# Two layer biases and the mask's alpha, added by accumulating DMAs instead of by VectorE

## The chip, the cores and the metric

The kernel runs on one core of one Trainium2 chip. The metric is the device time of one execution in microseconds (us); smaller is better. Time before: 1246.89 us, the median of 3 runs (1245.54 to 1247.73).

## What is computed

The input is x, 8 batches of 1024 nodes with 128 features in fp32, and one adjacency matrix adj, 1024 x 1024, mostly zero. Four graph layers follow one another, each with a residual and a layer norm:

```python
x = layernorm(x + (adj @ (x @ W0) + b0))                    # layer 0
x = layernorm(x + L1(x, adj))                               # layer 1: adj @ x and a rank-two term, @ W1, + b1
x = layernorm(x + L2(x, adj))                               # layer 2: attention
x = layernorm(x + L3(x, adj, 5 steps))                      # layer 3: gated recurrence
# layer 2
x_h = elu(x @ Wi + bi)
e = sigmoid(a_tgt[:, :, None] + a_src[:, None, :] + be)     # 1024 x 1024 for each batch
mask = adj + ALPHA * (1 - (adj != 0))                       # ALPHA = 0.005
e = e * mask
recv = elu(concat([e @ x_h, x_h * e.sum(-1)]) @ Wn + bn)
out = concat([recv, x_h]) @ Wm + bm
# layer 3, five times
m = adj @ h;  z = sigmoid(...m, h...);  r = sigmoid(...);  hv = tanh(...m, r*h...);  h = (1 - z)*h + z*hv
```

## The kernel before, in words

Products with adj are exact to about fp32: adj and x are split into a high and a low part (`adj_hi`, `adj_lo`, `xh`, `xl`), and each product is three passes of TensorE (`adj_product`, L700). One 128 x 1024 row tile of adj^T is loaded into each of eight buffers, `stage[0..7]` (fh, fr, fk, fz, hT0, hT1, r, v), which later hold the attention's and the recurrence's data. ScalarE makes `adj_hi` from a stage, VectorE `adj_lo`.

The **mask** of layer 2 is made from the same stages. VectorE computes `noedge = (stage == 0) * ALPHA` (L1237) into two slots of the ring, then `stage = stage + noedge` in place (L1239), and SyncE (the queue SP) stores the stage to a scratch in DRAM, `mask_scratch` (L621). SP loads no piece of the mask before all eight stores are in (`s_mstore`), and ScalarE waits for the same before its first attention copy, `t2a:0`, since that overwrites fh.

The four recurrences' pairs of batches (0 and 1, 2 and 3, 4 and 5, 6 and 7) run one after another. A pair has 5 steps of 2 batches, so there are 40 **units**, 0 to 39. A unit's TensorE work is two state products of 24 matmuls (128x512) and its gates. Layers 0 to 2 of each batch are cut into **pieces**, and `TABLES` at the head of the file lists for each engine in which order it runs them: lines `first` run ahead of unit 0, a line `unit5 @7 y0a:4` puts piece y0a of batch 4 into slot 7 of unit 5. Every engine runs its own list strictly in order and waits on semaphores for what it needs. The pieces that matter here (b is the batch):

- `x0` splits x (ScalarE, VectorE L1177). `m0a, m0b` are layer 0's adj products (half a and half b of the nodes, 24 matmuls each), `m1a, m1b` layer 1's. ScalarE copies each out of PSUM.
- `c0` (VectorE, L1258): x += b0 over 128 x 1024, after `xl0`. `c2`: x += bm, likewise, after ScalarE has copied the turned x (`tca`, `tcb`). `y0, y1, y2`: TensorE's small products (L718), and VectorE adds them to x (L1265); y0 waits for c0's, y2 for c2's signal.
- `v0, v1, v2` are norm statistics on VectorE (L1185 to L1203), `n0, n1, n2` the power -1/2 and a product on GpSimd (L659, L661) and eight applications on ScalarE (L979). n0 is followed by a new split: `xh1` on ScalarE, `l1` on VectorE.
- `d1` is two sets of row dots on VectorE (L1207), `sums` and `rows` the rank-two term of layer 1 (TensorE L759, L766, VectorE L1280 to L1298).
- Attention: `t2` turns x (L711), `pj` is x @ Wi with its elu (L778; VectorE L1305, L1308), `th` and `tg` (L711, L789), `as` (row dots). `s00..s17` are the 16 tiles of e: a sigmoid on ScalarE (L1029), on VectorE a product with a mask piece (L1326) and a running sum (L1333); `e00..e17` is the product on TensorE (L797). A mask piece (`k00..k17`) is loaded by SP into one of RING = 3 slots. `rs`, `rv`, `y2` end the attention.

The first list holds all of layers 0 and 1 of batches 0 to 2 and most of the attention of batches 0 and 1. GpSimd (POOL) has three loads of small vectors, the constants, and then only the n pieces and the output norms.

Of the kernel before, what the change touches and what calls it, by code (L numbers as in the profile page):

```python
# [81 lines left out]
unit0 @2 e10:1 e11:1 e12:1 @5 e13:1 @6 e14:1 e15:1 @7 e16:1 @8 pja:2 pjb:2 m1a:3 e17:1 m1b:3 rsa:1 sums:3 rsb:1 tha:2 rows:3 y1a:3 rva:1 y1b:3 @10 thb:2 tga:2 rvb:1 tgb:2 @13 y2a:1 @15 y2b:1 @20 e00:2 e01:2 e02:2 @25 e03:2 e04:2 e05:2 e06:2
unit1 @10 e07:2 @22 rsa:2 e10:2 e11:2 rva:2
unit2 @8 y2a:2 @15 e12:2 @22 e13:2 e14:2 e15:2
unit3 @22 e16:2 e17:2 rsb:2
unit4 @12 rvb:2 @21 y2b:2 @25 t2a:3
unit5 @13 t2b:3 pja:3 pjb:3 @18 tha:3 @19 thb:3 tga:3 @25 tgb:3
unit6 @11 e00:3 e01:3 @17 e02:3 @21 e03:3 @22 e04:3 e05:3
unit7 @11 e06:3 e07:3 @13 rsa:3 @22 e10:3
unit8 @6 e11:3 @9 e12:3 e13:3 e14:3 rva:3 @21 y2a:3 @22 e15:3 e16:3 e17:3  # L90
unit9 @27 rsb:3
unit10 @2 rvb:3 @10 y2b:3 @18 m0a:4 @20 m0b:4
unit11 @1 y0a:4 @3 y0b:4 @22 m1a:4 @24 m1b:4
unit12 @9 sums:4 @13 rows:4 @18 y1a:4 @21 y1b:4
unit13 @10 t2a:4 t2b:4 @12 pja:4 pjb:4 @17 tha:4 @18 thb:4 tga:4 m0a:5 tgb:4 m0b:5 e00:4 e01:4 @22 e02:4 e03:4 e04:4 y0a:5 e05:4
unit14 @2 e06:4 @6 y0b:5 e07:4 @8 rsa:4 @10 rva:4 e10:4 @15 e11:4 @16 e12:4 @19 y2a:4 e13:4 m1a:5 e14:4 @21 e15:4
unit15 @11 m1b:5 @12 e16:4 e17:4 sums:5 rsb:4 @13 rows:5 @14 rvb:4 @15 y1a:5 @19 y1b:5 y2b:4
unit16 @10 t2a:5 t2b:5 @16 pja:5 pjb:5 @21 tha:5 @22 thb:5 tga:5 @26 tgb:5
unit17 @10 e00:5 @11 e01:5 @17 e02:5 @18 e03:5 @19 e04:5 e05:5 @23 e06:5 @24 e07:5 @26 rsa:5 e10:5 e11:5
unit18 @1 rva:5 e12:5 e13:5 @8 y2a:5 e14:5 e15:5 e16:5 @9 e17:5 @11 rsb:5 @15 rvb:5 @22 y2b:5  # L100
# [4 lines left out]
unit23 @10 t2a:6 t2b:6 @13 pja:6 pjb:6 @17 m0a:7 tha:6 thb:6 m0b:7 tga:6 tgb:6 y0a:7 @19 y0b:7 @21 e00:6 @22 e01:6
unit24 @8 e02:6 e03:6 e04:6 @11 e05:6 @14 m1a:7 e06:6 @16 e07:6 @18 rsa:6 @22 m1b:7 rva:6 @26 sums:7
unit25 @12 rows:7 e10:6 e11:6 e12:6 y2a:6 @22 y1a:7 e13:6 e14:6
unit26 @1 e15:6 @3 y1b:7 e16:6 e17:6 @5 rsb:6 @10 rvb:6 @19 y2b:6 @23 t2a:7 t2b:7
unit27 @13 pja:7 pjb:7 @18 tha:7 @19 thb:7 tga:7 @22 tgb:7
unit28 @1 e00:7 @9 e01:7 @11 e02:7 @17 e03:7 @18 e04:7 @19 e05:7 e06:7 @23 e07:7 @25 rsa:7 e10:7 e11:7 @26 e12:7 @27 rva:7 e13:7 e14:7  # L110
# [19 lines left out]
unit1 @0 s07:2 @6 e07:2 s10:2 s11:2 s12:2 @8 s13:2 s14:2 @11 rva:2  # L130
unit2 @6 s15:2 @8 s16:2 s17:2
unit3 @8 e17:2
unit4 @6 rvb:2 @16 n2:2
unit5 @6 t2a:3 t2b:3 pja:3 pjb:3 tha:3 @8 thb:3 tga:3 @11 tgb:3 s00:3 @16 s01:3 s02:3
unit6 @6 s03:3 s04:3 s05:3 @8 s06:3 @10 s07:3
unit7 @6 e07:3 s10:3 s11:3 s12:3 @10 s13:3 @16 s14:3
unit8 @5 s15:3 s16:3 s17:3 rva:3 @11 e17:3
unit9
unit10 @1 rvb:3 @6 x0:4 m0a:4 n2:3 @11 m0b:4
unit11 @6 n0:4 @10 m1a:4 @11 m1b:4  # L140
unit12 @16 n1:4
unit13 @6 t2a:4 t2b:4 x0:5 pja:4 pjb:4 tha:4 @7 thb:4 tga:4 m0a:5 tgb:4 s00:4 s01:4 s02:4 m0b:5 s03:4 s04:4 @10 s05:4 s06:4 s07:4 @16 e07:4 s10:4 s11:4
unit14 @3 s12:4 @6 n0:5 rva:4 s13:4 @7 s14:4 @9 s15:4 s16:4 s17:4 m1a:5
unit15 @6 m1b:5 @7 e17:4 rvb:4 @16 n1:5
unit16 @6 n2:4 t2a:5 t2b:5 pja:5 pjb:5 @8 tha:5 @11 thb:5 tga:5 @12 tgb:5 @16 s00:5 s01:5 s02:5
unit17 @6 s03:5 s04:5 s05:5 s06:5 @8 s07:5 @11 e07:5 s10:5 s11:5 @12 s12:5 s13:5 s14:5 @16 rva:5 s15:5 s16:5
unit18 @3 s17:5 @5 e17:5 @6 rvb:5 @16 n2:5
unit19
unit20 @6 x0:6 @11 m0a:6 @12 m0b:6
# [2 lines left out]
unit23 @6 x0:7 t2a:6 t2b:6 pja:6 pjb:6 @7 m0a:7 tha:6 thb:6 m0b:7 tga:6 tgb:6 s00:6 @9 s01:6 s02:6 @10 s03:6 s04:6
unit24 @3 s05:6 n0:7 @6 s06:6 s07:6 @7 e07:6 s10:6 s11:6 s12:6 m1a:7 @10 m1b:7 rva:6
unit25 @6 s13:6 s14:6 s15:6 @10 s16:6 s17:6 @16 e17:6
unit26 @6 n1:7 rvb:6 @16 n2:6
unit27 @6 t2a:7 t2b:7 pja:7 pjb:7 tha:7 @8 thb:7 tga:7 @11 tgb:7 s00:7 @16 s01:7 s02:7
unit28 @5 s03:7 s04:7 @6 s05:7 s06:7 s07:7 @11 e07:7 s10:7 s11:7 s12:7 s13:7 s14:7 @12 s15:7 @16 rva:7 s16:7 s17:7
# [18 lines left out]
first s06:1 s07:1
unit0 @0 y0a:3 y0b:3 s10:1 s11:1 s12:1 v0:3 s13:1 s14:1 s15:1 s16:1 c2:2 l1:3 @2 s17:1 d1:3 pja:2 pjb:2 rsa:1 sums:3 rsb:1 rows:3 rva:1 y1a:3 y1b:3 as:2 rvb:1 v1:3 y2a:1 s00:2 s01:2 s02:2 y2b:1 v2:1 @4 s03:2 s04:2 s05:2 @9 s06:2
unit1 @0 s07:2 @4 s10:2 s11:2 s12:2 rsa:2 @6 s13:2 @7 s14:2 rva:2
unit2 @1 y2a:2 @4 s15:2 @6 s16:2 @7 s17:2
unit3 @7 rsb:2  # L180
unit4 @4 rvb:2 @6 y2b:2 @7 v2:2
unit5 @4 c2:3 pja:3 pjb:3 @6 as:3 @7 s00:3 @15 s01:3
unit6 @4 s02:3 s03:3 s04:3 s05:3 @6 s06:3 @7 s07:3
# [1345 lines left out]
```

## Time and profile before

| | |
|---|---|
| median of 3 runs | 1246.89 us (1245.54 to 1247.73) |
| the profiled execution | 1247.9 us, its span 1246.1 us |
| TensorE busy | 1200.8 us, 96% of the span |
| VectorE busy | 902.5 us, 72% |
| ScalarE busy | 678.7 us, 54% |
| GpSimd busy | 74.8 us, 6% |
| mean granted TensorE clock | 0.989 |

The span is the time from the first to the last instruction; 1.8 us of the profiled execution lie around it. Busy times of engines overlap, so what matters is where TensorE stands idle, and which engine's late result ends that idle time. A granted clock of 1.00 is TensorE at 2.4 GHz, and 0.5 would be 1.2 GHz; a stretch between the two spent part of its time at each.

### The profile page before, as it was taken

The numbers are of one execution on the slowest core, as the hardware profiler recorded it, in microseconds if no ns is written. First come the engines' busy times: TensorE is split into PE (matmuls) and PEld (weight loads), VectorE is DVE, ScalarE is ACT, GpSimd is POOL, SyncE is SP. The second block draws the span as 40 slices with busy tenths as digits, with TensorE's granted clock in tenths as the row PEclk, the third lists the DMA queues.
The fourth block names the chain that finished last, engine by engine and source line by source line (L and its number), as shares of the span: only waits on it lengthen the run. The fifth ranks groups of instructions, "written<-read, shape, count | busy, mean of one in ns | idle before, by whom it ended". The sixth has DMA issues, their size and how long they took to land.

```text
span 1246.1 us, 15438 instructions
## 1 busy us (share of the span) xinstructions
PE 1200.8 (96%) x5296; PEld 917.8 (74%) x5296; DVE 902.5 (72%) x2085; ACT 678.7 (54%) x1107; POOL 74.8 (6%) x79
## 2 busy tenths in 40 slices
...
GB/s 247 161 1 61 101 102 32 53 110 51 66 103 77 60 34 68 35 60 100 79 30 99 109 3 40 60 58 53 85 77 36 105 72 18 17 1 1 1 1 34
DMA packets 73038, 77.90 MB, mean 63 GB/s; under 512 B 6592, under 2 KB 48064, under 8 KB 72960
## 3 DMA queue, kind: packets, MB, share of 16 engines
...
## 4 chain that ended last, share of the span: by engine, by line
PE 77%; DVE 10%; ACT 4%; issue 3%; SPq 2%; DMA 2%; POOL 1%; DVEq 0%; POOLq 0%; ACTq 0%
PE ps L700 43%; PE ps L705 6%; PE ps L707 6%; PE ps L706 6%; PE ps L797 4%; PE ps L718 4%; PE ps L711 2%; DVE ring L1326 2%; DMA tl<-state_scratch 2%; ACT x L979 1%; SPq L588 1%; PE ps L810 1%; PE ps L778 1%; PE ps L803 1%; PE ps L789 1%
## 5 line engine op out<-in xcount | busy, mean ns | idle before, releaser
L700 PE MATMUL ps<-adj_hi,xh 128*128 128x512 f32 x672 | 288.5, 429 | 8.5 <-DVE xl L1177 6.2
L700 PE MATMUL ps<-adj_hi,xl 128*128 128x512 f32 x672 | 264.5, 394 | 0.0
L700 PE MATMUL ps<-adj_lo,xh 128*128 128x512 f32 x672 | 264.0, 393 | 0.0
L700 PEld LDWEIGHTS ps<-adj_hi,xh 128*128 128x128 f32 x672 | 127.6, 190 | 46.4 <-issue 16.0
L700 PEld LDWEIGHTS ps<-adj_lo,xh 128*128 128x128 f32 x672 | 127.7, 190 | 34.8 <-issue 11.3
L700 PEld LDWEIGHTS ps<-adj_hi,xl 128*128 128x128 f32 x672 | 127.3, 189 | 27.9
L797 PE MATMUL ps<-ring,fz 128*128 128x512 f32 x224 | 110.9, 603 | 3.5 <-DVE ring L1326 3.5
L1351 DVE TENSOR_TENSOR r<-r,hT 128x512 f32<-128x512 f32 x80 | 54.1, 690 | 78.7 <-ACT r L1089 78.5
L705 PE MATMUL ps<-mh,wh 128*128 128x512 f32 x240 | 104.2, 434 | 2.0 <-DVE ml L1177 1.5
L1177 DVE TENSOR_TENSOR ml<-ps,mh 128x512 fp32r<-128x512 f32 x80 | 55.0, 688 | 69.4 <-ACT mh L974 69.4
L974 ACT ACTIVATE mh<-ps 128x512 fp32r<-128x512 f32 x80 | 47.2, 591 | 104.2 <-PE ps L700 103.9
L1326 DVE TENSOR_TENSOR ring<-ring,mk 128x512 f32<-128x512 f32 x128 | 86.8, 682 | 21.6 <-ACT ring L1029 21.4
L1029 ACT ACTIVATE ring<-fh,asrcm 128x512 f32<-128x512 f32 x112 | 76.9, 718 | 39.0 <-PE ps L797 33.7
L707 PE MATMUL ps<-ml,wh 128*128 128x512 f32 x240 | 93.9, 391 | 0.0
L706 PE MATMUL ps<-mh,wl 128*128 128x512 f32 x240 | 93.6, 390 | 0.0
L974 ACT ACTIVATE xh<-tl 128x512 fp32r<-128x512 f32 x48 | 30.2, 630 | 99.7 <-DMA tl<-state_scratch 99.7
L1089 ACT ACTIVATE r<-ps,cols 128x512 f32<-128x512 f32 x80 | 54.5, 688 | 40.8 <-PE ps L707 40.5
L705 PE MATMUL ps<-th,wh 128*128 128x512 f32 x160 | 70.9, 443 | 2.7 <-DVE tl L1177 2.7
L1081 ACT ACTIVATE z<-ps,cols 128x512 f32<-128x512 f32 x80 | 53.6, 685 | 28.1 <-PE ps L707 27.8
L797 PEld LDWEIGHTS ps<-ring,fz 128*128 128x128 f32 x224 | 40.3, 190 | 38.7 <-issue 16.8
L1333 DVE TENSOR_TENSOR fr<-fr,ring 128x512 f32<-128x512 f32 x84 | 58.2, 692 | 8.8
L707 PE MATMUL ps<-tl,wh 128*128 128x512 f32 x160 | 62.6, 391 | 0.0
...
## 6 DMA issues: line engine op xcount, KB each, us to landing
mk<-mask_scratch SPq DMA_DIRECT2D x128, 256.0 KB, 2.8
...
x<-in_x SPq DMA_DIRECT2D x8, 512.0 KB, 4.1
out<-x SPq DMA_DIRECT2D x7, 512.0 KB, 3.2
hT<-in_adjT SPq DMA_DIRECT2D x2, 512.0 KB, 10.4
mask_scratch<-hT SPq DMA_DIRECT2D x2, 512.0 KB, 2.6
fh<-in_adjT SPq DMA_DIRECT2D x1, 512.0 KB, 5.0
```

The lines of the kernel that those rows point to most:

```text
L700: mm = pe.matmul(dst, a[:, t, :], b[:, t, cut(h)], start=(t == 0 and i == 0), stop=(t == T - 1 and i == 2))
L705: pe.matmul(dst, wh[:, k, :], hi, start=first, stop=False, skip_group_check=True)
L706: pe.matmul(dst, wl[:, k, :], hi, start=False, stop=False, skip_group_check=True)
L707: return pe.matmul(dst, wh[:, k, :], lo, start=False, stop=last, skip_group_check=True)
L797: tell(pe.matmul(ps[:, BANKS_B[b][h], :], f["z"][:, tile(t)], ring[:, place[b, h, t] % RING, :], start=(t == 0), stop=(t == T - 1)), "ag" ...
L974: return act.activation(dst, src, ACT.Copy)
L1029: tell(act.activation(ring[:, k % RING, :], f["h"][:, cut(h)], ACT.Sigmoid, bias=f["asrc"][:, t:t + 1]), "sg" + name[1:], b)
L1089: act.activation(r[:, cut(h)], ps[:, GB + h, :], ACT.Sigmoid, bias=rb).then_inc(r_done, 1)
L1177: return dve.tensor_tensor(dst, src, hi.bitcast(F32), ALU.subtract)
L1326: tell(dve.tensor_tensor(ring[:, k % RING, :], ring[:, k % RING, :], mk[:, k % RING, :], ALU.mult), "ma" + name[1:], b)
L1333: tell(dve.tensor_tensor(f["r"][:, cut(h)], first_sum, ring[:, k % RING, :], ALU.add), "rs_" + name[1:], b)
L1351: dve.tensor_tensor(r[:, cut(h)], r[:, cut(h)], hT[s][:, cut(h)], ALU.mult).then_inc(rh_done, 1)
```

## The change

- The VectorE pieces c0 and c2 are gone. GpSimd's queue issues for each of them a DMA that adds to x in SBUF (`accum_op=ALU.add`) from a scratch in DRAM, `bias_dram`, in which two small DMAs at the start repeat b0 and bm eight times to a row of 1024. y0 and y2 wait for the DMA's semaphore (`biased`).
- The mask: SP stores each raw stage to `mask_scratch` right after the weights' loads. VectorE waits for that store and then turns the stage in place into `(stage == 0) * ALPHA` (one instruction for two). GpSimd's queue issues a DMA that adds the stage to `mask_scratch`; its landing counts in `s_mstore`.
- GpSimd no longer waits for the last `adj_lo` before its list.
- All five lists are written anew: the order of pieces in `first` and their unit and slot.

```diff
     "PE": """
-first m0a:0 m0b:0 y0a:0 y0b:0 m0a:1 m0b:1 y0a:1 m0a:2 m1a:0 m1b:0 sums:0 y0b:1 m0b:2 rows:0 y1a:0 y0a:2
-first y0b:2 y1b:0 m1a:1 m1b:1 sums:1 t2a:0 t2b:0 rows:1 y1a:1 y1b:1 pja:0 pjb:0 m1a:2 tha:0 thb:0 m1b:2
-first tga:0 tgb:0 t2a:1 sums:2 t2b:1 rows:2 pja:1 e00:0 y1a:2 e01:0 e02:0 pjb:1 y1b:2 e03:0 e04:0 e05:0
...
+first m0a:0 m0b:0 m0a:1 y0a:0 y0b:0 m0b:1 y0a:1 y0b:1 m0a:2 m0b:2 m1a:0 m1b:0 sums:0 m1a:1 rows:0 y1a:0
+first m1b:1 y1b:0 sums:1 y0a:2 y0b:2 rows:1 y1a:1 y1b:1 t2a:0 t2b:0 pja:0 pjb:0 tha:0 thb:0 tga:0 tgb:0
+first m1a:2 t2a:1 m1b:2 e00:0 e01:0 e02:0 e03:0 t2b:1 e04:0 sums:2 pja:1 e05:0 e06:0 e07:0 rows:2 y1a:2
...
     "ACT": """
-unit0 @0 e07:1 s10:1 s11:1 s12:1 t2a:2 t2b:2 @1 s13:1 s14:1 s15:1 @2 s16:1 n0:3 @4 s17:1 pja:2 pjb:2 e17:1 m1a:3 m1b:3 tha:2 rva:1 thb:2 tga:2 rvb:1 tgb:2 s00:2 s01:2 s02:2 n1:3 @8 s03:2 s04:2 s05:2 @9 n2:1 @11 s06:2
+unit0 @0 s16:1 s17:1 t2a:2 e17:1 t2b:2 pja:2 pjb:2 @1 n0:3 rva:1 tha:2 @2 thb:2 m1a:3 rvb:1 m1b:3 @4 tga:2 tgb:2 s00:2 s01:2 s02:2 n2:1 @8 s03:2 s04:2 n1:3 @9 s05:2 @10 s06:2 @11 s07:2
...
     "DVE": """
-first x0:0 c0:0 x0:1 x0:2 y0a:0 c0:1 y0b:0 weights:0 v0:0 mask:0 c0:2 mask:1 y0a:1 mask:2 l1:0 d1:0 mask:3
-first mask:4 mask:5 mask:6 mask:7 y0b:1 sums:0 v0:1 rows:0 y0a:2 y1a:0 y1b:0 l1:1 v1:0 d1:1 y0b:2 v0:2
...
+first x0:0 x0:1 x0:2 weights:0 mask:0 mask:1 mask:2 mask:3 mask:4 mask:5 y0a:0 y0b:0 mask:6 v0:0 y0a:1 y0b:1
+first mask:7 v0:1 l1:0 d1:0 l1:1 d1:1 sums:0 rows:0 y1a:0 y1b:0 v1:0 sums:1 y0a:2 y0b:2 rows:1 v0:2 y1a:1
+first y1b:1 v1:1 pja:0 pjb:0 l1:2 as:0 d1:2 s00:0 s01:0 s02:0 s03:0 s04:0 s05:0 s06:0 s07:0 sums:2 pja:1
...
-unit18 @1 s16:5 s17:5 y2a:5 @4 rsb:5 rvb:5 @7 y2b:5 v2:5
-unit19
-unit20 @5 x0:6 @9 c0:6 @13 y0a:6 @15 y0b:6 v0:6
+unit18 @4 pja:5 pjb:5 @7 as:5 @15 s00:5
+unit19 @4 s01:5 s02:5 s03:5 s04:5 @5 s05:5 s06:5 s07:5 @9 s10:5 s11:5 @10 s12:5 s13:5 @13 s14:5 @15 rsa:5 s15:5 s16:5 s17:5 rva:5
+unit20 @2 y2a:5 rsb:5 x0:6 @4 rvb:5 y2b:5 v2:5 @11 y0a:6 @15 y0b:6 v0:6
...
     "POOL": """
-first n0:0 n0:1 n1:0 n0:2 n1:1 n1:2 n2:0 n0:3 n1:3 n2:1 n2:2
+first c0:0 c0:1 c0:2 mask:0 mask:1 mask:2 mask:3 mask:4 mask:5 mask:6 n0:0 mask:7 n0:1 n1:0 c2:0 n0:2 n1:1
+first c2:1 n1:2 c0:3 n2:0 c2:2 n0:3 n2:1 n1:3 n2:2 c2:3 n2:3
...
+        def biased(b, n):
+
+            return s_xb[b // 2 % 2][b % 2], 32 * (b // 4) + (16 if n == "0" else 32)
...
-            for n, t in enumerate(t for piece, t in order["DVE"] if piece == "mask"):
-                sp.wait_ge(s_mask, n + 1)
-                sp.dma_start(mask_dram[tile(t), :], stage[t]).then_inc(s_mstore, 16)
+            for t in range(T):
+                sp.wait_ge(s_adj[t], 16)
+                sp.dma_start(mask_dram[tile(t), :], stage[t]).then_inc(s_adj[t], 16)
...
+            for n, c in enumerate((0, 2)):
+                pool.dma_start(bias_dram[n:n + 1, :].rearrange("o (t d) -> o t d", d=D),
+                               w["rows"][:, c * D:(c + 1) * D].unsqueeze(1).to_broadcast([1, T, D])
+                               ).then_inc(s_rep, 16)
...
+                if name == "mask":
+                    pool.wait_ge(s_mask, 1 + [t for piece, t in order["DVE"] if piece == "mask"].index(b))
+                    pool.dma_start(mask_dram[tile(b), :], stage[b], accum_op=ALU.add).then_inc(s_mstore, 16)
                     return
                 f = set_of(name, b)
-                if name in ("n0", "n1", "n2"):
+                if name in ("c0", "c2"):
+                    pool.wait_ge(s_rep, 32)
+                    for e in ("xl0",) if name == "c0" else ("tca", "tcb"):
+                        seen(pool, e, b)
+                    n = int(name == "c2")
+                    pool.dma_start(x_of(b)[:, :, :].rearrange("p t d -> p (t d)"),
+                                   bias_dram[n:n + 1, :].to_broadcast([P, N]), accum_op=ALU.add
+                                   ).then_inc(biased(b, name[1])[0], 16)
+                elif name in ("n0", "n1", "n2"):
...
-            pool.wait_ge(s_al, T)
...
             def mask(t):
...
                 dve.wait_ge(s_al, t + 1)
-                dve.tensor_scalar(noedge, stage[t], 0.0, ALPHA, ALU.is_equal, ALU.mult).then_inc(s_noedge, 1)
-                dve.wait_ge(s_noedge, n + 1)
-                dve.tensor_tensor(stage[t], stage[t], noedge, ALU.add).then_inc(s_mask, 1)
+                dve.wait_ge(s_adj[t], 32)
+                dve.tensor_scalar(stage[t], stage[t], 0.0, ALPHA, ALU.is_equal, ALU.mult).then_inc(s_mask, 1)
...
-                elif name in ("c0", "c2"):
-                    row, before = ((b0b, ("xl0",)) if n == "0" else (bmb, ("tca", "tcb")))
-                    dve.wait_ge(s_wv, 16 * V_LOADS)
-                    for e in before:
-                        seen(dve, e, b)
-                    tell(dve.tensor_tensor(x[:, :, :], x[:, :, :], row.unsqueeze(1).to_broadcast([P, T, D]), ALU.add),
-                         "xb" + n, b)
                 elif name in ("y0a", "y0b", "y1a", "y1b", "y2a", "y2b"):
                     h = "ab".index(name[2])
-                    seen(dve, ("xb0", "kbx", "xb2")[int(n)], b)
+                    if n == "1":
+                        seen(dve, "kbx", b)
+                    else:
+                        dve.wait_ge(*biased(b, n))
```

## Rows read from the trace of the kernel before

**Rows 1.** The span in seven windows: length, busy us (count) of each engine, PEclk, DMA share, GB/s
```profile
0.00:22.00 22.00, 13.14 (x48) 10.39 (x48) 13.30 (x11) 12.73 (x12) 2.80 (x14) 1.00 0.95 308
22.00:60.00 38.00, 37.16 (x188) 31.71 (x189) 33.56 (x100) 9.05 (x18) 2.99 (x3) 1.00 0.39 147
60.00:105.00 45.00, 40.29 (x204) 32.89 (x203) 33.25 (x163) 21.89 (x47) 7.38 (x8) 0.92 0.02 9
105.00:187.00 82.00, 75.01 (x284) 44.08 (x283) 70.24 (x161) 60.05 (x93) 8.10 (x6) 0.98 0.32 100
187.00:240.00 53.00, 48.70 (x216) 35.24 (x216) 38.19 (x131) 24.12 (x44) 4.64 (x4) 0.94 0.14 45
240.00:1215.00 975.00, 969.37 (x4290) 751.03 (x4290) 694.35 (x1460) 538.31 (x873) 44.74 (x40) 1.00 0.17 55
1215.00:1246.10 31.10, 17.08 (x76) 12.47 (x74) 19.64 (x61) 12.55 (x24) 4.12 (x5) 0.82 0.12 35
```

**Rows 2.** Waits of TensorE from 60 to 240 us: us in total, times, longest
```profile
PE ps L700 <- DVE xl L1177: 6.2, 2, 3.2
```

**Rows 3.** Chain of waits, 0 to 260 us: start us, us, what
```profile
68.23 14.05 PE ps L700 x48
...
91.09 5.48 PE ps L700 x24
...
223.05 1.50 ACT x L979 x4
```

**Rows 4.** VectorE's instruction groups by shape: count, busy us, mean ns, idle before
```profile
L1258 DVE TENSOR_TENSOR x<-x,rows 128x1024 f32<-128x1024 f32 x16 | 19.3, 1209 | 0.4 <-ACT fh L974 0.4
L1239 DVE TENSOR_TENSOR hT<-hT,ring 128x1024 f32<-128x1024 f32 x2 | 2.5, 1227 | 0.1
L1237 DVE TENSOR_SCALAR ring<-hT 128x1024 f32<-128x1024 f32 x2 | 1.4, 694 | 0.1
```

**Rows 5.** Timeline of SyncE's queue at the start: start us, us, what
```profile
20.55 0.44 SPq L618 DMA_DIRECT2D mk<-in_u  x1
...
54.08 0.32 SPq L621 DMA_DIRECT2D mask_scratch<-v  x1
57.46 176.60 SPq L577 DMA_DIRECT2D mk<-mask_scratch  x43
```

**Rows 6.** DMA issues: count, KB each, median us to landing
```profile
mask_scratch<-hT SPq DMA_DIRECT2D x2, 512.0 KB, 2.6
...
v<-in_adjT SPq DMA_DIRECT2D x1, 512.0 KB, 12.4
...
rows<-in_rows POOLq DMA_DIRECT2D x1, 384.0 KB, 8.0
```

**Rows 7.** Timeline of GpSimd: start us, us, what
```profile
2.52 0.54 POOL L640 DMA_DIRECT2D rows<-in_rows  x1
...
32.25 1.95 POOL L659 TENSOR_TENSOR rsAm<-veAm,mhalf 128x8 f32<-128x8 f32 x1 [28.16 <-DVE veAm L1203]
...
59.81 1.64 POOL L659 TENSOR_TENSOR rsAa<-veAa,mhalf 128x8 f32<-128x8 f32 x1 [24.68 <-DVE veAa L1203]
```

**Rows 8.** Timeline of ScalarE: start us, us, what
```profile
35.17 3.19 ACT L979 ACTIVATE x<-x,nbAm,rsAm 128x128 f32<-128x128 f32 x8 [4.19 <-POOL nbAm L661]
38.39 1.07 ACT L974 ACTIVATE fxh<-x 128x1024 fp32r<-128x1024 f32 x1
...
107.05 0.72 ACT L1029 ACTIVATE ring<-fh,asrcm 128x512 f32<-128x512 f32 x1
```

**Rows 9.** Timeline of VectorE: start us, us, what
```profile
57.24 1.64 DVE L1185 BATCH_NORM_STATS2 stAa<-x 128x6 f32<-128x128 f32 x8
...
59.57 0.17 DVE L1203 TENSOR_TENSOR veAa<-veAa,mvAa 128x8 f32<-128x8 f32 x1
61.63 2.16 DVE L1292 SCALAR_TENSOR_TENSOR x<-ps,svm,x 128x128 f32<-128x128 f32 x8 [1.89 <-PE ps L766]
...
186.32 0.69 DVE L1333 TENSOR_TENSOR r<-r,ring 128x512 f32<-128x512 f32 x1
```

More of the change, by code:

```diff
@@ L82 @@
[L82 to L100, printed above, removed]
-unit19
-unit20 @21 m0a:6 @26 m0b:6
-unit21 @1 y0a:6 @3 y0b:6 @22 m1a:6 @24 m1b:6
-unit22 @2 sums:6 @14 rows:6 @21 y1a:6 @22 y1b:6
@@ L105 @@
[L105 to L110, printed above, removed]
@@ new lines @@
+first e01:1 y2a:0 rsb:0 e02:1 e03:1 e04:1 rvb:0 e05:1 e06:1 e07:1 m0a:3 y2b:0 e10:1 e11:1 e12:1 m0b:3 e13:1
+first e14:1 e15:1 y0a:3 y0b:3 e16:1 t2a:2 e17:1 t2b:2 pja:2 rsa:1 pjb:2
+unit0 @2 rsb:1 @4 tha:2 rva:1 thb:2 @7 m1a:3 rvb:1 m1b:3 y2a:1 sums:3 y2b:1 rows:3 y1a:3 @8 tga:2 tgb:2 y1b:3 @19 e00:2 @20 e01:2 @21 e02:2 @22 e03:2 @24 e04:2 @25 e05:2 e06:2 e07:2 rsa:2
+unit1 @10 rva:2 @22 y2a:2 e10:2 @25 e11:2
+unit2 @11 e12:2 e13:2 @22 e14:2 e15:2 e16:2
+unit3 @11 e17:2 @13 rsb:2 @15 rvb:2 @22 y2b:2
```

219 lines of the change are left out of this document (118 added, 101 removed).

## The prediction

> **What bounds the kernel now.** I read the windows first [rows 1]. TensorE is busy 969.4 of the 975 us from 240 to 1215 us, so over four fifths of the span a faster VectorE can return at most the 5.6 us that are left. The last 31 us (14.0 us idle) and the first 22 (8.9 idle, with the DMA engines 95% busy) belong to the ending and to the loading of adj. That leaves 22 to 240 us: 0.8 us idle to 60, 4.7 to 105, 7.0 to 187, 4.3 to 240, together 16.8 us. There VectorE is busy 33.6 of 38, 33.3 of 45, 70.2 of 82 and 38.2 of 53 us, and is the engine that comes late: the waits of TensorE name its xl twice, 6.2 us in all and 3.2 the longer [rows 2].
>
> A long wait costs twice. In the chain [rows 3] a run of 48 matmuls after the first xl wait takes 14.05 us where 24 take 5.48 later: 3.1 us more than twice that. The granted clock of the windows shows it too [rows 1]: 0.92 in 60 to 105, 0.98 in 105 to 187, 0.94 in 187 to 240, against 1.00 in the others from 22 to 1215. A clock at its lower level (0.5) for a part f of a window gives 1 - f/2, so TensorE ran at 1.2 GHz for 0.16 x 45 = 7, 0.04 x 82 = 3 and 0.12 x 53 = 6 us, and lost half of each, 8 us in all. The most that a perfect feed from 22 to 240 could return is 16.8 + 8, about 25 us. The matmuls themselves are the same before and after.
>
> **What is removed.** Sixteen bias additions of 1.21 us (19.3 us) and eight mask additions of 1.23 us (9.8 us) [rows 4]. The eight mask comparisons of 0.69 us stay. VectorE loses 29 of 902 us. By the lists, c0 of batches 0 to 3, c2 of 0 and 1 and all masks stood before unit 0: 6 x 1.21 + 8 x 1.23 = 17.1 us less there. The other ten biases are 12.1 us, one (c2:2) in unit 0 and nine beside a TensorE that idles 5.6 us in 975; I give those no gain.
>
> **What is added, and what covers it.**
> - Two small repeats and 24 accumulating DMAs of 512 KB on GpSimd's queue. Issuing one costs GpSimd about 0.54 us, as the load of rows did [rows 7]; GpSimd is busy 75 us in all, so 26 x 0.54 = 14 us fit, except where a norm piece stands behind them. n0:0 now stands behind seven mask DMAs, which follow the masks at 0.7 us each, so little is added: 0 to 1 us.
> - The landing of an accumulating DMA is in no row. From below, a plain store of 512 KB lands in 2.6 us; from above, the last adj tile, in a full queue, took 12.4 us [rows 6]. It reads two operands and writes one where a copy reads one, so I take 5.2 us, twice the undisturbed row. A c0 has the two halves of m0 (2 x 5.5 us) before y0 needs it, and a c2 the whole attention. Both are hidden up to the upper end.
> - Eight raw stores, 4 MB, directly behind the last weight load (issued at 20.55) instead of from 33.96 on by the masks' pace; the last one was issued at 54.08 and the mask's first load at 57.46 [rows 5]. At the 308 GB/s of the first window 4 MB take 13.6 us, so the last stages are stored at about 35 and VectorE's comparisons run behind them.
> - c0:0 transfers while adj and x still load at 0.95 DMA share: 1 MB more read or written at 308 GB/s is up to 3.4 us, of which TensorE, which waits on the tiles only at the start, may see 0 to 1.5. Against it stands the gap after m0:0 that closes (the 0.8 us of the second window). Sum of both: -1 to +1.5, taken +0.5.
>
> **The new order, walked** with the pieces' durations. TensorE leaves m0b:0 at about 22 and has m0a:1, m0b:1, m0a:2, m0b:2 (4 x 5.5) and four small y0 (under 1 each) before m1a:0, which is due at 47. VectorE has the weights until 29, six comparisons and two y0 sums to about 35.5, and v0:0, which is 2.5 us [rows 9], to 38; GpSimd needs 2 to 2.8 more, ScalarE 3.2 + 1.1 [rows 8], VectorE 1.2 for l1:0: 46 to 47. No stall, but no slack either; 0 to 2 us, taken 0.
>
> From there to 105 I find two waits. t2a:0 waits for n1:0 (rows:0, y1, v1:0 and the norm behind one another): 2 us. And pja:0 stands on VectorE behind rows:1 (3.5 us), v0:2, the y1 sums and v1:1 (2.5 each for the norms), so tha:0 waits 4.5 us at about 85. With 0.6 at rows:1 that is 7.1 us against the 4.7 before: +2.4 us, with the clock's loss about the same as before (one long wait in each). On the other side VectorE is ahead: s00's sigmoid starts at about 98 instead of 107.05 [rows 8].
>
> From 105 to the end of s17:1 VectorE has a queue of 32 tiles at 2 x 0.69 = 1.4 us and some 21 us of others, without c0:3 and c2:1: from 98 that ends at 164, with the same 7 us of gaps as before at 171, where it ended at 187 [rows 9]. TensorE's 75.0 busy us of that window [rows 1] held unit 0's first product (5.5) and parts of batch 3's layer 1 and of the gates' neighbours that the new list puts later; I count some 61 us for it from 105 on, through at 166 at best, so 0.5 to 5 us idle remain of 7.0: -4 us, with both ends -6.5 and -2.
>
> In unit 0 the wait for batch 1's split (3.2 us, xl, [rows 2]) has n2:1 (ScalarE, 223.05, [rows 3]) ahead of the reset gate. It moves into an earlier slot, but n1:3, as long (3.2), takes a slot between the two update gates. Part of the wait and of the clock loss behind it stays: of 4.3 + 3 us I take 3 back (0 to 7).
>
> **Sum.** +0.5 + 2.4 - 4 - 3 = -4.1 us. Against the profiled execution, 1247.9, that is 1243.8; the median of the runs is 1.0 lower, 1246.89, and so I predict **1242.8 us**. A measurement can tell about 0.2%, 2.5 us, from no change.
>
> **A rule against it.** Between GpSimd's power of 1.95 us beside VectorE's mask work and 1.64 us beside an idle VectorE lie 0.3 us [rows 7]: it was held up a little. The Trainium skill (SBUF — State Buffer, "SBUF: two separate sides") says that GpSimd can't write the descriptors of its DMAs while VectorE runs an instruction in a mode with two ports. By that rule each mask DMA would start up to 0.7 us later, in sum nothing on TensorE's path. The Trainium skill (Collectives: The Full Stack, "The bandwidth ceiling") states that a reduction reads twice per byte written and runs at about half a copy's rate; no row here shows it. By that rule the doubling above would hold, and the sum would not change.
>
> **The rivals.**
> 1. *The time is given back* (same, 0.22). TensorE has the same matmuls, and the list's new waits before 105 are as long as those it removes later. With the waits at their upper bounds (+1.5, +4.4, -2, -1) it ends at +3, with the middle ones near 0: 1247.
> 2. *Slow accumulation* (slower, 0.15). All eight mask DMAs must land before ScalarE may copy t2a:0, and TensorE's list stands behind that, at about 81. The first is issued at about 29.5. If they pass one after another, 8 x T = 52 us gives the point from which it decides: T = 6.5 us. At 8 us it costs 12 us, 1255; at 12.4, the upper bound, 47. For it: GpSimd's queue and the double reading are in no row, and three c0 go ahead of them. Against it: at the first window's 308 GB/s a transfer of 512 KB takes 1.7 us of the DMA engines' time, and twice that is 3.4, well under 6.5 [rows 1].
> 3. *The early waits grow* (slower, 0.12). n0:0 comes late behind the mask DMAs, TensorE stalls at 47 and again at 85, each time with a slow clock behind it: 2 + 3 + 3 us more, 1250. Against it: each engine's slack above.
> 4. *The full gain* (faster, 0.13): the stalls before 105 do not come, the tile stage runs without waits and unit 0 closes: -5, -6, -6: 1233.
> That a bias is not added in time to matter is no case of its own: y0 and y2 wait for it.
>
> **How the numbers follow.** The forecast itself (-2.5 to -9 us) has 0.38. Faster is 0.38 + 0.13 = 0.51; same 0.22; slower 0.27. The range goes from 1236, which leaves out most of rival 4, to 1254, which takes in rival 3 and the near part of rival 2.
>
> **What would show it.** VectorE busy at 873 of the span, TensorE's busy time near 1199; idle of TensorE between 22 and 240 at 12 us; no wait of ScalarE for mask DMAs; a landing of accumulating DMAs under 6.5 us; s17:1's sum near 171; the waits at t2a:0 and tha:0. Wrong it is if the windows from 240 on show over 10 us idle (unit 20, where batch 5's norm now ends late, is the place to look), or if a wait for `mask_scratch` or for a bias stands ahead of TensorE.

## The result and the profile after

The changed kernel takes **1281.93 us** (1280.98 to 1283.21, 4 runs); the kernel before, run beside it, 1247.24 (1245.54 to 1247.73, 4 runs). The ratio is 1.0281 [1.0269, 1.0293]: slower by 35 us, where 1242.8 was forecast and 1254 was the upper end. The profiled execution has a span of 1279.4 us, 33.3 more than before.

Busy times and queues, from the page of the changed kernel (the two q rows: packets, MB, share of the time of 16 DMA engines):

```profile
PE 1205.5 (94%) x5296; PEld 920.3 (72%) x5296; DVE 873.5 (68%) x2061; ACT 676.7 (53%) x1105; POOL 96.2 (8%) x105
...
q1 hardware_dynamic: 72816, 76.51, 18.7%
q0 software_dynamic: 3664, 12.99, 5.5%
```

VectorE is down to 873.5 us, as the diff says. TensorE's idle time rose from 45.3 (1246.1 - 1200.8) to 73.9 us (1279.4 - 1205.5), by 28.6, and its busy time by 4.7 though the matmuls are the same: the clock, whose mean went from 0.989 to 0.982. The two make the 33.3.

The seven windows of [rows 1] and what is left of the span:

```profile
0.00:22.00 22.00, 13.19 (x46) 10.68 (x47) 10.94 (x9) 11.51 (x11) 4.84 (x17) 1.00 0.94 304
22.00:60.00 38.00, 26.57 (x132) 21.87 (x130) 17.31 (x54) 7.43 (x16) 11.81 (x13) 0.90 1.07 278
60.00:105.00 45.00, 36.99 (x196) 30.80 (x196) 28.79 (x144) 14.94 (x30) 5.43 (x7) 0.93 0.15 37
105.00:187.00 82.00, 72.77 (x268) 43.59 (x269) 65.69 (x189) 56.08 (x90) 9.17 (x8) 0.96 0.38 109
187.00:240.00 53.00, 51.98 (x251) 38.40 (x250) 36.73 (x138) 28.13 (x51) 8.27 (x7) 1.00 0.12 33
240.00:1215.00 975.00, 953.29 (x4180) 734.92 (x4179) 676.93 (x1444) 531.10 (x865) 52.61 (x49) 0.99 0.21 61
1215.00:1246.10 31.10, 31.10 (x146) 25.73 (x145) 15.56 (x23) 14.80 (x23) 0.00 (x0) 1.00 0.00 1
1246.10:1279.40 33.30, 19.60 (x85) 14.34 (x83) 21.54 (x65) 12.67 (x24) 4.12 (x5) 0.82 0.11 32
```

Two rows carry the loss. From 22 to 60 us TensorE idles 11.4 us (0.8 before), the clock is 0.90, VectorE is busy only 17.3 of 38 us, and the DMA share went from 0.39 to 1.07. From 240 to 1215 it idles 21.7 us (5.6 before); 3.9 of them lie between 240 and 260 us and still belong to the start, which has moved over the window's edge (187 to 240 idles 1.0 us where it idled 4.3). The waits of TensorE name who was late (us, times, longest):

```profile
PE ps L720 <- DVE fxl L1197: 12.8, 1, 12.8
...
PE ps L809 <- ACT fz L994: 7.1, 4, 3.3
PE ps L720 <- ACT fm L994: 6.8, 2, 4.0
PE ps L731 <- DVE fk L1317: 4.6, 2, 4.2
```

**The first place** is m1a:0, which waits 12.8 us for the split of batch 0 after its norm (fxl). The timeline of VectorE shows why; L1252 is the mask's comparison, and the brackets give idle time and what ended it:

```profile
31.49 0.69 DVE L1252 TENSOR_SCALAR fr<-fr 128x1024 f32<-128x1024 f32 x1
36.24 0.69 DVE L1252 TENSOR_SCALAR fk<-fk 128x1024 f32<-128x1024 f32 x1 [4.06 <-DMA mask_scratch<-fk]
40.06 0.69 DVE L1252 TENSOR_SCALAR fz<-fz 128x1024 f32<-128x1024 f32 x1 [3.13 <-DMA mask_scratch<-fz]
43.88 0.69 DVE L1252 TENSOR_SCALAR hT<-hT 128x1024 f32<-128x1024 f32 x1 [3.13 <-DMA mask_scratch<-hT]
47.67 0.70 DVE L1252 TENSOR_SCALAR hT<-hT 128x1024 f32<-128x1024 f32 x1 [3.10 <-DMA mask_scratch<-hT]
48.28 1.28 DVE L1274 TENSOR_TENSOR x<-ps,x 128x512 f32<-128x512 f32 x2
...
61.05 1.22 DVE L1197 TENSOR_TENSOR fxl<-x,fxh 128x1024 fp32r<-128x1024 f32 x1 [2.25 <-ACT fxh L994]
```

VectorE may not overwrite a stage before its raw copy is stored, and these stores land one per 3.8 us. The sums of y0:0 stand behind six comparisons in its list and start at 48.3, where I had them before 35.5, and v0:0 stands behind a seventh. The chain of waits goes through the store that this one waits for, and the DMA issues (KB each, us to landing) show the stores and what shared the engines with them:

```profile
28.07 23.33 DMA mask_scratch<-r
```
```profile
mask_scratch<-fh SPq DMA_DIRECT2D x1, 512.0 KB, 5.5
mask_scratch<-fr SPq DMA_DIRECT2D x1, 512.0 KB, 7.6
...
mask_scratch<-r SPq DMA_DIRECT2D x1, 512.0 KB, 23.3
mask_scratch<-v SPq DMA_DIRECT2D x1, 512.0 KB, 25.7
mask_scratch<-fh POOLq DMA_DIRECT2D x1, 512.0 KB, 10.1
```

Here a store takes up to 25.7 us against the 2.6 of [rows 6]. Part of that is the queue of its own kind: eight stores are issued within 6.3 us, and without the three c0 beside them (e10, below) the last takes 11.0 us.

**The second place** is four stalls of 2.8, 3.3, 4.0 and 3.1 us in the windows from 560, 700, 860 and 1000 us, 20 us each. The state of the recurrence goes through DRAM (48 stores of 256 KB, each fetched back in four pieces of 64 KB), and where a bias DMA is on its way at that moment the fetch is late. The third of them in the chain, the instruction of ScalarE that waited, and GpSimd at that time:

```profile
859.15 3.69 DMA state_scratch<-v
...
864.53 7.36 DMA tl<-state_scratch
...
873.17 8.14 PE ps L720 x24
```
```profile
871.92 0.63 ACT L994 ACTIVATE xh<-tl 128x512 fp32r<-128x512 f32 x1 [9.73 <-DMA tl<-state_scratch]
872.45 0.58 ACT L994 ACTIVATE fm<-ps 128x512 f32<-128x512 f32 x1
```
```profile
859.98 0.92 POOL L674 DMA_DIRECT2D x<-bias_scratch  x1 [8.40 <-ACT fh L994]
862.87 1.02 POOL L674 DMA_DIRECT2D x<-bias_scratch  x1 [1.98 <-DVE fxl L1197]
```

GpSimd issued two bias DMAs at 859.98 and 862.87; ahead of each of the other three stalls one or two were issued too, 6 to 10 us before it begins. The fetch of 64 KB took 7.4 us (median 2.0). ScalarE, in its written order, waits in front of xh, the copy that empties PSUM (fm) stands behind it, and TensorE waits for that. It costs 4.0 us, and 24 matmuls then take 8.14 us where 5.48 is the undisturbed time [rows 3]; the granted clock is 1.00 from 865 to 870 us and 0.50, that is 1.2 GHz, from 873 to 876.

### The profile page after: what moved, and what is told of

Read it like the earlier page. It is cut to its first block, busy times and chain, and to the rows that moved or that the text cites. A ratio compares the mean times of both kernels' runs of the same rounds, so it can differ in the third digit from the quotient of the medians.

```text
span 1279.4 us, 15440 instructions
## 1 busy us (share of the span) xinstructions
PE 1205.5 (94%) x5296; PEld 920.3 (72%) x5296; DVE 873.5 (68%) x2061; ACT 676.7 (53%) x1105; POOL 96.2 (8%) x105
## 3 DMA queue, kind: packets, MB, share of 16 engines
q1 hardware_dynamic: 72816, 76.51, 18.7%
q0 software_dynamic: 3664, 12.99, 5.5%
## 4 chain that ended last, share of the span: by engine, by line
PE 69%; DVE 11%; ACT 7%; DMA 5%; SPq 3%; issue 3%; POOL 1%; DVEq 0%; POOLq 0%; ACTq 0%
PE ps L720 37%; PE ps L725 6%; PE ps L727 6%; PE ps L726 6%; PE ps L817 5%; PE ps L738 3%; DMA tl<-state_scratch 3%; ACT x L999 3%; DMA mask_scratch<-r 2%; PE ps L731 2%; DVE ring L1335 2%; DVE hT L1381 1%; ACT th L994 1%; SPq L593 1%; PE ps L779 1%
## 5 line engine op out<-in xcount | busy, mean ns | idle before, releaser
L720 PEld LDWEIGHTS ps<-adj_lo,xh 128*128 128x128 f32 x672 | 126.5, 188 | 35.4 <-issue 12.5
L720 PE MATMUL ps<-adj_hi,fxh 128*128 128x512 f32 x144 | 60.2, 418 | 19.6 <-DVE fxl L1197 12.8
L1197 DVE TENSOR_TENSOR xl<-tl,xh 128x512 fp32r<-128x512 f32 x48 | 33.0, 687 | 48.7 <-ACT xh L994 48.5
```

Source lines behind the costliest of these rows:

```text
L720: mm = pe.matmul(dst, a[:, t, :], b[:, t, cut(h)], start=(t == 0 and i == 0), stop=(t == T - 1 and i == 2))
L1197: return dve.tensor_tensor(dst, src, hi.bitcast(F32), ALU.subtract)
```

## The experiments

Thirteen variants, each timed beside the kernel before. "Idle" is TensorE's in the windows 22 to 60 and 240 to 1215 us (window less busy time).

| run | order | mask | biases | us | ratio | idle 22-60 | idle 240-1215 |
|---|---|---|---|---|---|---|---|
| before | old | VectorE | VectorE | | | 0.8 | 5.6 |
| after | new | DMA | DMA | 1281.9 | 1.0281 [1.0269, 1.0293] | 11.4 | 21.7 |
| e3 | new | VectorE | VectorE | 1255.7 | 1.0064 [1.0049, 1.0079] | 7.1 | 7.0 |
| e4 | new | VectorE | DMA | 1275.7 | 1.0232 [1.0199, 1.0265] | 8.9 | 21.2 |
| e1 | old | DMA | VectorE | 1247.2 | 1.0006 [0.9995, 1.0017] | 0.7 | 5.8 |
| e2 | old | VectorE | DMA | 1263.1 | 1.0127 [1.0106, 1.0147] | 2.3 | 15.7 |
| e5 | old | none | none | 1247.4 | 0.9999 [0.9988, 1.0009] | 0.7 | 6.0 |
| e6 | new | none | none | 1246.5 | 0.9996 [0.9986, 1.0005] | 0.0 | 6.5 |
| e7 | old | VectorE | VectorE, plain copies beside | 1253.7 | 1.0056 [1.0038, 1.0073] | 1.4 | 8.1 |
| e8 | old | VectorE | DMA, some late | 1261.1 | 1.0110 [1.0094, 1.0125] | 2.2 | 14.9 |
| e9 | new, n0 first | DMA | DMA | 1271.3 | 1.0191 [1.0172, 1.0209] | 5.5 | 19.3 |
| e10 | new | DMA | VectorE | 1245.9 | 0.9992 [0.9980, 1.0003] | 0.0 | 4.4 |
| e11 | old | VectorE | DMA, behind the state | 1255.2 | 1.0063 [1.0041, 1.0085] | 2.6 | 11.3 |
| e12 | new | DMA | DMA, not c0:0 to 2 | 1269.4 | 1.0164 [1.0130, 1.0198] | 0.0 | 18.1 |
| e13 | new | DMA | c0:3, c2:0 to 3 | 1247.6 | 1.0003 [0.9990, 1.0016] | 0.0 | 5.8 |

In the runs whose start is late, part of the last column is still the start's: between 240 and 260 us the changed kernel idles 3.9 us, e4 3.9, e3 3.1, e9 2.6 and e1 1.2, the others under 0.4. Less that, the changed kernel has 17.8 us late, e4 17.3, e12 18.1, and e3 3.8.

### One part at a time: order, mask, biases

**e3**, the new lists with all the work on VectorE:

```diff
-first x0:0 x0:1 x0:2 weights:0 mask:0 mask:1 mask:2
+first x0:0 c0:0 x0:1 c0:1 x0:2 c0:2 weights:0 mask:0 mask:1 mask:2
```

> The new order of pieces with all sixteen biases and the mask on VectorE as before (c0 right behind x0, c2 right before pja). Theory A (the DMAs cost the time: the mask's stores and accumulating DMAs crowd the start, the bias DMAs crowd the state's trip through DRAM later): within 5 us of before, and TensorE idle between 240 and 1215 us back near 6 us. Theory B (the new order costs it): 1265 to 1280.

1255.7 us, between the ranges of the two theories. TensorE waits 7.1 us for fxl: six masks at 1.9 us (comparison and addition) now stand ahead of y0:0 in VectorE's list. So the new order has a cost of its own as long as the mask stays on VectorE. Late in the units nothing is lost (7.0 us idle for 5.6, 3.1 of them the start's).

**e4**, the same with the biases by DMA (on GpSimd as in the change, y0 and y2 wait for `biased`):

```diff
-first x0:0 c0:0 x0:1 c0:1 x0:2 c0:2 weights:0 mask:0
+first x0:0 x0:1 x0:2 weights:0 mask:0
+                    pool.dma_start(x_of(b)[:, :, :].rearrange("p t d -> p (t d)"),
+                                   bias_dram[n:n + 1, :].to_broadcast([P, N]), accum_op=ALU.add
```

> The changed kernel with only the mask taken back to VectorE (two instructions and one store per tile). Theory A: the 11 us idle of 22 to 60 us shrink to under 3, the late stalls before mh, fm and fz copies that wait for the state's landing stay: 1258 to 1266. Theory B: as the changed kernel, less at most 5.

1275.7 us, 20 more than e3, and late idle 21.2 for 7.0. The late stalls come with the bias DMAs, not with the order. The time lies above the 1258 to 1266 given and the idle time from 22 to 60 stayed at 8.9 us instead of under 3: the order's own wait, which e3 shows, was not in that expectation.

**e1**, the old lists and only the mask by DMA:

```diff
+            for t in range(T):
+                sp.wait_ge(s_adj[t], 16)
+                sp.dma_start(mask_dram[tile(t), :], stage[t]).then_inc(s_adj[t], 16)
...
+                    pool.dma_start(mask_dram[tile(b), :], stage[b], accum_op=ALU.add).then_inc(s_mstore, 16)
```

> The order of before, only the mask by raw stores and accumulating DMAs. Theory A: no late stall (idle 240 to 1215 near 6 us); at the start v0:0 stands ahead of the masks but l1:0 behind three of them, so TensorE stalls some 5 to 10 us before m1a:0 and the total is 1252 to 1265. Theory B: within 3 us of before.

1247.2 us, no difference. The expectation of a loss was a miss: the raw stores land in 5.5 to 11.8 us and VectorE waits for none. The eight mask additions alone are free.

**e2**, the old lists and only the biases by DMA:

```diff
-first x0:0 c0:0 x0:1 x0:2 y0a:0 c0:1 y0b:0 weights:0
+first x0:0 x0:1 x0:2 y0a:0 y0b:0 weights:0
...
+                        dve.wait_ge(*biased(b, n))
```

> The order of before, only the biases by accumulating DMAs (GpSimd: c0 ahead of its n0, c2 as soon as the turned x is copied). Theory A: some state fetches land in 4 to 7 us instead of 2, TensorE idles 10 to 16 us in 240 to 1215: 1255 to 1265. Theory B: within 3 us of before, as the order is before's.

1263.1 us: the biases alone cost 1.3%, and of TensorE's 11.1 us more idle time 10.1 lie after 240 us. Once VectorE does wait for a bias here, 2.4 us at a sum of layer 0. The part of the change that I had thought fully covered by other work is the one that costs.

### What there was to gain

**e5** and **e6**: the old and the new lists, without biases of layers 0 and 2 and without alpha, by no engine at all (the comparisons are left out too, and the raw adjacency is stored as the mask):

```diff
             def mask(t):
+                return
...
                 if name in ("c0", "c2"):
+                    return
```

> The order of before, with neither biases of layers 0 and 2 nor the mask's alpha anywhere: the raw adjacency is stored as the mask and y0, y2 add without bias. It shows the most that taking this work off VectorE could return. If VectorE's 29 us stood in TensorE's way, 1230 to 1240; if they were covered, 1243 to 1248.

> The new order with the same parts left out (no biases of layers 0 and 2, no alpha). If the new order is good once the work is gone, it beats the bare old order by 3 us or more (1235 to 1242), as my walk had it; if the order's waits at 85 us and at unit 0 are as long as those they replace, both bare kernels are within 3 us.

1247.4 and 1246.5 us, both the same as before. Waits of TensorE in e5, beside [rows 2]:

```profile
PE ps L730 <- DVE xl L1207: 6.2, 2, 3.2
```

32.5 us of VectorE's work are gone (902.5 - 870.0) and the very same wait, of the same length, stands there. What became of the time is seen at one sum of VectorE, before and then in e5:

```profile
55.80 0.69 DVE L1265 TENSOR_TENSOR x<-ps,x 128x512 f32<-128x512 f32 x1 [1.74 <-PE ps L718]
```
```profile
55.63 0.69 DVE L1289 TENSOR_TENSOR x<-ps,x 128x512 f32<-128x512 f32 x1 [13.37 <-PE ps L748]
```

It waits for TensorE in both, and starts at the same time. In the new order the stalls are others (6.9, 7.5 and 3.8 us idle in the windows from 60, 105 and 187) and their sum is no smaller. So taking this work off VectorE had nothing to win, in either of the two orders.

### What a bias DMA does to others

**e7**: biases on VectorE as before, and a plain copy of 512 KB from DRAM to DRAM on GpSimd's queue in each bias DMA's place:

```diff
+                    pool.dma_start(copy_dram[2 * b + n], bias_dram[n:n + 1, :].to_broadcast([P, N])
+                                   ).then_inc(s_copy, 16)
```

> Before with its biases on VectorE, and where the bias-only kernel issues an accumulating DMA, GpSimd issues a plain copy of the same 512 KB from the same scratch to another scratch in DRAM that nobody reads. If any transfer of that size beside the state's trip delays it: 1255 to 1265, with state fetches of 4 to 7 us. If it is the accumulation (two reads for one write): within 6 us of before, fetches at most 4.

1253.7 us, between the two ranges given. Transfers that nobody waits for cost 0.6%, so this part is the traffic (or GpSimd's time to issue it, 85.9 us busy for 74.8), not the wait for a result. The rest of e2's 1.3% goes with what the copy does not do: it adds nothing, writes to DRAM instead of SBUF, and no sum waits for it (2.4 us in e2). No run separates the three. For the same 8.80 MB GpSimd's queue takes 3.8% of the DMA engines' time in e2 and 2.4% in e7. The state's DMAs, issue to landing (min/median/max, us), in e7, then in e2:

```profile
DMA to landing us min/median/max: 1.8/2.1/5.1
```
```profile
DMA to landing us min/median/max: 1.8/2.1/7.7
```

The median does not move (before: 2.1, with a maximum of 4.0); a few fetches do, and those are on TensorE's path.

**e8** and **e11** move the late c2 away from the state's trip, in the old order. e8 lets those of batches 4 to 7 wait for a later product (ma02), e11 those of batches 3 to 7 until the unit's state is back; c0:5 and c0:7 go back to VectorE in both:

```diff
+                    if name == "c2" and b >= 4:
+                        seen(pool, "ma02", b)
```
```diff
+                    if name == "c2" and b in trip:
+                        pool.wait_ge(xh_done, nth_but(*trip[b]))
```

> The bias-only kernel in the order of before, with c2 of batches 4 to 7 held back until the third tile of the attention's product (after the state's trip of that unit) and c0 of batches 5 and 7 on VectorE. If the meeting with the state's trip is the cause, TensorE's idle time from 240 to 1215 falls from 15.7 to under 8 us and the total is 1246 to 1252. If accumulating DMAs cost wherever they stand: 1256 or more.

> The bias-only kernel in the order of before, with c2 of batches 3 to 7 held back until the state of the same unit has come back from DRAM (so that some 14 us pass before the next trip), and c0 of batches 5 and 7 on VectorE. If the meeting with the trip is all of the late cost: TensorE idle from 240 to 1215 at most 8 us, every state fetch under 5 us, total 1247 to 1253 (the start's loss of e2, about 2 us idle, stays). If it is not: 1256 or more.

e8, 1261.1 us, settles nothing: the shifted DMAs met other trips (one was issued at 680.5, and the window 680 to 700 idles 4.4 us; the state's longest landing is 7.3). e11, 1255.2 us, halves the cost of e2, and the longest landing is 3.9 us, as before (4.0). e8 has the same number of bias DMAs, so the 5.9 us between the two are a matter of when they run. But e11 lies in neither of the ranges given: it still loses 0.6%, and idles 11.3 us late, where at most 8 were expected. At y0:4 VectorE waits 2.3 us for a bias and TensorE 1.9, the start's 2.6 us stay, and the rest is spread over waits of under 1 us whose cause no run shows. So a late fetch is not the whole of what a late bias DMA costs in the old order.

### The start

**e9**, the changed kernel with n0:0 ahead of the mask additions on GpSimd:

```diff
-first c0:0 c0:1 c0:2 mask:0 mask:1 mask:2 mask:3 mask:4 mask:5 mask:6 n0:0 mask:7
+first c0:0 c0:1 c0:2 n0:0 mask:0 mask:1 mask:2 mask:3 mask:4 mask:5 mask:6 mask:7
```

> The changed kernel with one piece moved: on GpSimd n0:0 stands ahead of all eight mask accumulations instead of behind seven, so none starts before v0:0. If the accumulations are what slows the raw stores (one every 3.8 us instead of 1.7), the stores land by 36 to 42 us without them, VectorE's comparisons are through before that, and TensorE's wait of 12.8 us before m1a:0 shrinks to 0 to 5 us; total 1262 to 1272. If the raw stores alone, or the c0 additions, slow one another, the wait stays over 8 us.

1271.3 us, the wait for fxl is 4.4 instead of 12.8. The additions now start at 48 us, and the raw stores land in 5.5 to 14.3 us (23 and 26 in the changed kernel). With the three c0 alone beside them the stores are late already (fk after 12.1 us); with the mask additions as well, each released by the store before it, they fall into the 3.8 us beat. GpSimd's timeline of this run also shows issues that grow longer:

```profile
48.10 0.94 POOL L676 DMA_DIRECT2D mask_scratch<-fh  x1
...
49.29 1.54 POOL L676 DMA_DIRECT2D mask_scratch<-fk  x1
...
51.99 3.30 POOL L676 DMA_DIRECT2D mask_scratch<-v  x1
52.55 4.43 POOL L690 TENSOR_TENSOR rsAa<-veAa,mhalf 128x8 f32<-128x8 f32 x1
```

**e10**, the changed kernel with all biases on VectorE:

```diff
-first x0:0 x0:1 x0:2 weights:0 mask:0 mask:1 mask:2
+first x0:0 c0:0 x0:1 c0:1 x0:2 c0:2 weights:0 mask:0 mask:1 mask:2
...
-first c0:0 c0:1 c0:2 mask:0 mask:1 mask:2
+first mask:0 mask:1 mask:2
```

> The new order with the mask by DMA and all biases on VectorE. Without the three c0 accumulations in the start: if the mask's own accumulations slow the raw stores, the wait before m1a:0 stays at 8 us or more and the total is 1254 to 1262, no late stalls; if the c0 additions did it, the wait is under 4 us and the total 1247 to 1253.

1245.9 us, as fast as before, and 36 us faster than the changed kernel. The windows 22 to 60 and 105 to 187 us, and the running sums of VectorE's second line (the last starts at 176.4):

```profile
22.00:60.00 38.00, 38.00 (x193) 32.27 (x192) 27.22 (x121) 13.33 (x27) 12.30 (x12) 1.00 0.96 264
...
105.00:187.00 82.00, 73.32 (x280) 42.66 (x279) 67.45 (x158) 56.04 (x86) 7.38 (x6) 1.00 0.29 94
```
```profile
L1361 DVE TENSOR_TENSOR r<-r,ring x12: 691/692/694, 144.4 to 176.4; 128x512 f32<-128x512 f32 x12
```

The DMA share from 22 to 60 is 0.96, hardly less than the 1.07 of the changed kernel, and TensorE does not idle at all. The raw stores:

```profile
mask_scratch<-fr SPq DMA_DIRECT2D x1, 512.0 KB, 6.2
...
mask_scratch<-v SPq DMA_DIRECT2D x1, 512.0 KB, 11.0
```

A high share alone is no stall; what counts is that the stores that VectorE waits for land first.

### How the 36 us divide

**e12** takes c0:0, c0:1 and c0:2 back to VectorE, **e13** also both biases of batches 4 to 7 (the variants hold the pieces of GpSimd's DMAs in a list; what is not in it stands in VectorE's order, as in e10):

```diff
+        BY_DMA = ['c0:3', 'c0:4', 'c0:5', 'c0:6', 'c0:7', 'c2:0', 'c2:1', 'c2:2', 'c2:3', 'c2:4', 'c2:5', 'c2:6', 'c2:7']
```
```diff
+        BY_DMA = ['c0:3', 'c2:0', 'c2:1', 'c2:2', 'c2:3']
```

> The changed kernel, but the biases of x0:0, x0:1 and x0:2 are added by VectorE behind the sums; all other biases and the mask stay with the DMAs. If the three bias additions of the start are what slows the raw mask stores, TensorE is idle for under 1.5 us between 22 and 60 us (12.8 us in the changed kernel), the four stalls late in the units stay (13 us or so), and the time is 1262 to 1268 us. If they are not the cause, the wait ahead of m1a:0 stays over 5 us and the time is 1272 us or more.

> As the run before it, and the biases of the batches 4 to 7 (both layers) are also added by VectorE; the mask, c0:3 and c2:0 to c2:3 stay with the DMAs. If all that is left of the cost is the meeting of bias additions with the state's way through DRAM, TensorE is idle for no more than 7 us between 240 and 1215 us (the kernel before has 6 or so) and the time is 1246 to 1251 us. If the late stalls have another cause, they stay, and the time is 1256 us or more.

e12: 1269.4 us, 1.4 above the range given; the stall at the start is gone (0.0 us idle) and the four late ones stay. e13: 1247.6 us, the same as before. Waits of TensorE in e12, then in e13:

```profile
PE ps L819 <- ACT fz L1004: 9.5, 4, 2.8
...
PE ps L730 <- ACT fm L1004: 7.0, 2, 3.7
```
```profile
PE ps L819 <- ACT fz L1004: 3.5, 2, 1.9
```

And the windows from 240 us on, e12, then e13:

```profile
240.00:1215.00 975.00, 956.88 (x4212) 741.74 (x4211) 669.90 (x1433) 525.81 (x854) 52.58 (x49) 0.99 0.20 60
```
```profile
240.00:1215.00 975.00, 969.19 (x4303) 753.08 (x4302) 690.35 (x1457) 535.09 (x868) 45.00 (x41) 1.00 0.18 55
```

So of the changed kernel's 34.3 us over e13, 12.5 (1281.9 - 1269.4) are the three early biases and 21.8 the eight late ones, each to some 4 us: the four runs of e12 lie between 1264.3 and 1271.0. Of the spans' 20.5 us between e12 and e13, 12.4 are idle time (60.3 against 47.9) and 8.1 longer matmuls (busy 1206.0 against 1197.9): the clock behind the stalls costs two thirds as much again as the stalls. Five bias DMAs and all the mask's stay in e13 at no measurable cost.

## Why the prediction was wrong, point by point

- **What bounds the kernel.** Right as far as it went: TensorE's own work, and at most some 25 us outside. But "VectorE is the engine that comes late" was read as "VectorE's busy time matters". e5 takes 32.5 us away and returns nothing: VectorE's sums in front of xl wait for TensorE (13.4 us idle ahead of the one at 55.6, 1.9 ahead of the one at 61.5), so xl is late by what stands before it in the chain, not because VectorE is full.
- **The failed step: the added DMAs were put at nothing once their own landing was covered ("Both are hidden up to the upper end").** The cover was reckoned only for whether y0 and y2 get their bias in time. That much holds in the changed kernel, where no engine waits for a bias addition: the four late stalls are waits for ScalarE's copies. What was left out is what these DMAs do to the transfers beside them. VectorE's new wait for the raw stores was walked ("No stall, but no slack either; 0 to 2 us, taken 0"), with stores that had the engines to themselves; the state's fetch, which was on ScalarE's path all along, had no term at all. It should have been a row: 48 trips through DRAM that cost nothing as long as the longest landing is 4.0 us. Measured in the new order: +12.5 and +21.8 us, for 0 and 0.
- **"The last stages are stored at about 35."** The last landed at 29.5 + 25.7 = 55 us. 4 MB at 308 GB/s supposes the engines are the stores' own; with three c0 beside them, and then the mask additions, they were not: the DMA share from 22 to 60 us is 1.07. Without the c0 (e10) the last landed at 27.0 + 11.0 = 38 us, VectorE waited 1.5 and 0.5 us for two of them, and TensorE idles 0 us from 22 to 60, as walked. The walk of the order was good; the landing it stood on was not.
- **c0:0 beside the loads, 0 to +1.5.** I asked what it costs TensorE during the loading (nothing: 13.19 us busy to 22 us, as before), and not what it costs the stores behind: the first raw store is issued at 23.3 us, and at 20.8 in e10.
- **The landing of an accumulating DMA, 5.2 us.** Well sized for one that runs alone: 4.9 at 195 us. The sixteen of the changed kernel take up to 11.9, with a median of 6.7, above the 6.5 named as a sign. Issue was taken at 0.54 us from the load of rows and is 0.87 to 1.0, 0.4 us more each, on nobody's path here.
- **Early waits, +2.4.** tha:0's, forecast 4.5, is 4.2 (fk, above). The one at t2a:0, forecast 2, did not come (y1 waits 1.9 us for a term of layer 1 in its stead). In e6 the window idles 6.9 us, where 7.1 was forecast, but that is partly luck: tha:0 waits 3.0 us there, t2a:0 not at all, and y1's 2.0 were not foreseen.
- **-4 from 105 to 187, -3 in unit 0.** The last sum of s17:1, forecast to start at 171 instead of 187, starts at 176.4 in e10 and at 192.8 in the changed kernel, and the first sigmoid at 99.1 in e10 (forecast 98). VectorE did run ahead, but TensorE idles 8.7 us in that window of e10 and 7.0 before: it waits for other results of VectorE (fr, fh, ring, kbp). A faster VectorE is no gain where the next waits stand just behind. Both terms are near 0 in e6: the windows idle 7.5 us for 7.0 and 3.8 for 4.3.
- **The rivals.** None was this one, and 1281.9 us lies far above all of their middle values; only rival 2's upper bound (+47 us) reaches it. Rival 2 had the right sort of cause (DMA time) at the wrong place: it priced the mask additions against t2a:0, which nobody waited for in e1 and e10. Rival 3 named the right wait, m1a:0's behind n0:0, but priced it at 2 us, with GpSimd's queue as the cause, and the raw stores not at all. Rival 1, nothing is gained, describes e6 and e10, that is the change less its bias DMAs.
- **What I named as a sign of error came**: over 10 us idle from 240 us on. I had unit 20 and a wait for a bias in mind. It was state trips in other units.
- **The rules cited.** On the doubled cost: accumulating transfers took 5.5% of the engines' time for 12.99 MB and the others 18.7% for 76.51 MB, 1.7 times as much per MB, and in e9 eight queued additions land 2.9 us apart ((73.6 - 53.4) / 7), 1.7 times the 1.7 us that 512 KB take at 308 GB/s. The Trainium skill (Collectives: The Full Stack, "The bandwidth ceiling") says that a reduction runs at about half a copy's rate; that agrees roughly, as do e2 and e7 (3.8% against 2.4% for the same bytes, 1.6 times). The rule of the Trainium skill (SBUF — State Buffer, "SBUF: two separate sides") on GpSimd's descriptors held up by VectorE is not to be seen as a cost: e1 and e10 lose nothing.
